# QKV's last two blocks: x transposed by VectorE and DMA transfers in place of TensorE

## What is computed

```python
x = x + attention(layernorm(x), Wqkv, bqkv, Wo, bo)     # q, k, v of width 256
x = x + ffn(layernorm(x), gate_w, up_w, down_w, fc1_w, fc2_w, expert_w, gamma, beta)
```

## Time and profile before

| | us |
|---|---|
| median of 3 runs | 2321.71 |
| lowest and highest | 2320.19 and 2321.98 |
| the profiled execution | 2322.11 |
| its span (first to last instruction) | 2320.3 |

### The profile page before, as it was taken

One profiled execution on the slowest core, in us unless ns is written; L12 is line 12 of the kernel. 1 busy time (PEld: TensorE's weight loads), 2 busy tenths in 40 slices (PEclk: granted clock), 3 DMA queues, 4 the chain that ended last, 5 costly groups with the idle time before them and its releaser, 6 DMA issues.

```text
span 2320.3 us, 27515 instructions
## 1 busy us (share of the span) xinstructions
PE 2307.1 (99%) x10888; PEld 1939.1 (84%) x10888; DVE 1578.0 (68%) x1772; ACT 794.3 (34%) x885; POOL 281.0 (12%) x550
## 2 busy tenths in 40 slices
PE   9999999999999999999999999999999999999998
PEld 8988988888888878888888888888888888888886
DVE  7787649887989765598763378774249876424548
ACT  4333336666555441522221331213132121223211
POOL 3000000000223200033100023210003220000000
PEclk9999999999999999999999999999999999999999
DMA  8999854532334699978996678898668999666865
GB/s 309 333 359 363 300 193 164 198 122 80 122 120 144 224 314 334 317 276 313 342 308 197 191 275 299 312 335 262 193 219 274 320 331 320 209 193 206 239 209 194
DMA packets 232801, 580.83 MB, mean 250 GB/s; under 512 B 26208, under 2 KB 80096, under 8 KB 232288
## 3 DMA queue, kind: packets, MB, share of 16 engines
q1 hardware_dynamic: 151392, 443.52, 58.1%
q10 hardware_dynamic: 81280, 135.55, 16.0%
HBM read 421.96 MB, written 152.83 MB: 248 GB/s over the span
## 4 chain that ended last, share of the span: by engine, by line
PE 92%; DVE 3%; DMA 1%; SPq 1%; ACT 1%; issue 1%; POOL 1%; ACTq 0%; DVEq 0%; POOLq 0%
PE psum L1116 11%; PE psum L1117 11%; PE psum L1118 11%; PE psum L1095 10%; PE psum L1096 10%; PE psum L1097 10%; PE psum L930 3%; PE psum L928 3%; PE psum L929 3%; PE psum L968 2%; PE psum L998 2%; PE psum L970 2%; PE psum L969 2%; PE psum L1000 2%; PE psum L999 2%; PE psum L948 1%
## 5 line engine op out<-in xcount | busy, mean ns | idle before, releaser
L1751 DVE TENSOR_TENSOR HB<-HB,psum 128x1024 f32<-128x1024 f32 x135 | 163.0, 1217 | 299.1 <-PE psum L1097 299.1
L1972 POOL TENSOR_SCALAR veA<-mvA 128x1 f32<-128x1 f32 x32 | 31.2, 976 | 1269.0 <-DVE mvA L1659 1269.0
L1341 ACT ACTIVATE HB<-HB 128x1024 f32<-128x1024 f32 x64 | 67.8, 1060 | 307.6 <-DVE HB L1751 307.6
L1095 PE MATMUL psum<-XS2h,WR 128*128 128x512 f32 x280 | 109.4, 391 | 1.0 <-DVE XS2l L1457 0.7
L1095 PE MATMUL psum<-XS1h,WR 128*128 128x512 f32 x280 | 109.3, 390 | 0.3 <-DMA WR<-wu_s 0.2
L1095 PE MATMUL psum<-XS0h,WR 128*128 128x512 f32 x280 | 109.1, 390 | 0.0
L1095 PE MATMUL psum<-XS3h,WR 128*128 128x512 f32 x280 | 109.1, 390 | 0.0
L1097 PE MATMUL psum<-XS0h,WR 128*128 128x512 f32 x280 | 109.0, 389 | 0.0
L1096 PE MATMUL psum<-XS1l,WR 128*128 128x512 f32 x280 | 109.0, 389 | 0.0
L1096 PE MATMUL psum<-XS2l,WR 128*128 128x512 f32 x280 | 109.0, 389 | 0.0
L1097 PE MATMUL psum<-XS1h,WR 128*128 128x512 f32 x280 | 109.0, 389 | 0.0
(11 more groups left out here) (402 smaller groups left out, 6616.6 us busy)
## 6 DMA issues: line engine op xcount, KB each, us to landing
WR<-wu_s SPq DMA_DIRECT2D x280, 512.0 KB, 4.3
WR<-wd_s SPq DMA_DIRECT2D x280, 512.0 KB, 4.7
att_s<-ATT ACTq DMA_DIRECT2D x32, 516.0 KB, 3.4
RAW<-in_x_dram SPq DMA_DIRECT2D x32, 512.0 KB, 8.2
RES<-x1b_s SPq DMA_DIRECT2D x128, 128.0 KB, 5.6
out_dram<-ZR ACTq DMA_DIRECT2D x118, 128.0 KB, 5.5
xT_s<-XT SPq DMA_DIRECT2D x24, 512.0 KB, 7.5
HB<-xT_s SPq DMA_DIRECT2D x12, 1024.0 KB, 8.8
```

The source lines that it names most:

```text
L1095: e.matmul(o, w[:, 0, ws], h[:, :, ws], start=kt == 0, stop=False)
L1751: e.tensor_tensor(to, a, src, op=ALU.add).then_inc(*vevac.next(key))
```

## The change

Blocks 6 and 7 (`MOVED`) no longer have `xt_tr`, `xt_hi` and `xt_lo`. In their place:

- `x_turn` (VectorE), four a block at slots b, b, b+1, b+1 with b = 12 (u - 1): transposes the 32x32 squares of one normalised tile of `RAW` into `XAT`, which is the memory of the low part of `XA[u % 2]`. It waits for the V products of block u - 2.
- `x_move` (SP) at b+2: 16 transfers of 32 partitions by 4 KB from `XAT` back into `RAW`, behind the last `x_turn`.
- `x_parts` at b+7 to b+10: high part (ScalarE) and low part (VectorE), read from `RAW` in runs of 32 numbers; both wait for all 16 transfers.

Since `RAW` is now in use until the last `x_parts`, all that waited for the last transpose of a block waits for its last low part (`raw_done`), and the quads d(1,0), d(1,1), d(2,0) and the loads and splits of q go one to three slots later. V's products of block 5 and 6 no longer wait for the transposes of the next block to be read out of their banks.

```diff
+MOVED = (6, 7)
@@ timetable
+        if u in MOVED:
+            for tt in range(4):
+                at(b + tt // 2, "x_turn", u, tt)
+            at(b + 2, "x_move", u)
+            for a in range(4):
+                at(b + 7 + a, "x_parts", u, a)
+            continue
         for a in range(4):
             at(b + 2 * a, "xt_tr", u, a)
             at(b + 2 * a, xt_out, u, a, b + 2 * a + 1)
-    for q, n0, times in ((("d", 1, 0), 68, (70, 71, 72, 72, 72, 73)), (("d", 1, 1), 75, (77, 78, 79, 79, 79, 80)),
-                         (("d", 2, 0), 82, (85, 86, 87, 87, 87, 88)), (("d", 2, 1), 84, (86, 87, 88, 88, 88, 89)),
+    for q, n0, times in ((("d", 1, 0), 71, (73, 74, 75, 75, 75, 76)), (("d", 1, 1), 78, (80, 81, 82, 82, 82, 83)),
+                         (("d", 2, 0), 85, (88, 89, 90, 90, 90, 91)), (("d", 2, 1), 84, (86, 87, 88, 88, 88, 89)),
...
-        at((80, 80, 86, 86)[j], "q_load_a", j // 2, j % 2)
-        at((84, 85, 89, 90)[j], "q_split_a", j // 2, j % 2)
+        at((83, 83, 88, 88)[j], "q_load_a", j // 2, j % 2)
+        at((86, 87, 90, 91)[j], "q_split_a", j // 2, j % 2)
@@ memory
+    XAT = [at(f"XA{i}t", [128, 4, 8, 4, 32], F32, 128.5 + 32 * i) for i in range(2)]
@@ ScalarE
+        def x_parts(u, a):
+            on.wait_ge(*xm_in[u])
+            src, h, _ = moved(u, a)
+            high(h, src, "xt", u, a)
@@ VectorE
+        def x_turn(u, tt):
+            on.wait_ge(*v_mm[u - 2, 3])
+            on.wait_ge(*normed[u, tt])
+            e.transpose(XAT[u % 2][:, :, :, tt, :].rearrange("p m k r -> p k m r"),
+                        RAW[u % 2][:, tt, :].rearrange("p (k m c) -> p k m c", k=8, m=4)).then_inc(*normed.next(("turn", u, tt)))
+
+        def x_parts(u, a):
+            src, h, l = moved(u, a)
+            low(l, src, h, "xt", u, a)
@@ SyncE
+        def x_move(u):
+            on.wait_ge(*normed["turn", u, 3])
+            for g, m in itertools.product(range(4), range(4)):
+                src = XAT[u % 2][32 * g:32 * g + 32, m].rearrange("p k t r -> p (k t r)")
+                e.dma_start(RAW[u % 2][32 * m:32 * m + 32, g, :], src).then_inc(
+                    *xm_in.next(*((u,) if g == m == 3 else ()), by=16))
```

More of the change, by code:

```diff
@@ L741, in transformer_layer @@
     wq_in, wv_in = [landed(f"wq{n}") for n in range(4)], landed("wv")
+    xm_in = landed("xm")
     bq_in, gr_in, bv_in = landed("bq"), landed("gr"), landed("bv")
@@ L802, in xt_bank, with raw_done, moved @@
         return 2 * (a % 2) if u == 0 else 6 - 2 * (a % 2)
+    def raw_done(u):
+        return lo["xt", u, 3] if u in MOVED else xt_mm[u, 3]
+    def moved(u, a):
+        src = RAW[u % 2][:, :, 256 * a:256 * a + 256].rearrange("p g (q r) -> p g q r", r=32)
+        return (src, *(q[:, 2 * a:2 * a + 2, :].rearrange("p k n -> p (k n)").rearrange("p (q g r) -> p g q r", q=8, g=4)
+                       for q in XA[u % 2]))
     def v_bank(t, tt):
@@ L939, in pe_v @@
             if t == 7:
-                on.wait_ge(*(vevac["v", 6, 3] if tt < 2 else lo["xt", 7, 2]))
-            elif tt < 2:
+                on.wait_ge(*(vevac["v", 6, 3] if tt < 2 else lo["xt", 5 if 7 in MOVED else 7, 2]))
+            elif tt < 2 or t + 1 in MOVED:
                 on.wait_ge(*(vevac["v", t - 1, tt] if t else lo["xt", 0, 3]))
@@ L1553, in P_acc @@
                 on.wait_ge(*exps[i, 1])
-                on.wait_ge(*(rs_mm[i - 1] if i else xt_mm[7, 3]))
+                on.wait_ge(*(rs_mm[i - 1] if i else raw_done(7)))
                 e.tensor_tensor(acc[:, :], SA[:, sa(i, 0), :], s, op=ALU.add).then_inc(*acc_s.next((1, i)))
@@ L1944, in vector @@
         do = {"e_split": e_split, "f_split": f_split, "wq_split": wq_split, "wv_split": wv_split, "load_qkv": load_qkv,
-              "ln_stats": ln_stats, "ln_norm": ln_norm, "e2_out": e2_out, "xt_lo": xt_lo, "v_out": v_out,
+              "ln_stats": ln_stats, "ln_norm": ln_norm, "e2_out": e2_out, "xt_lo": xt_lo, "x_turn": x_turn, "x_parts": x_parts, "v_out": v_out,
               "kv_split": kv_split, "q_split_a": q_split_a, "q_split": q_split, "mx_op": mx_op, "m_fold": m_fold,
@@ L2084, in q_load_a @@
             on.wait_ge(*qk_stored(i, d))
-            on.wait_ge(*(lo["q", i - 1] if i else xt_mm[7, 3]))
+            on.wait_ge(*(lo["q", i - 1] if i else raw_done(7)))
             e.dma_start(STQ[:, d, :], qk_s[i, d]).then_inc(*stq_in[d].next(i, by=16))
@@ L2124, in quad_load @@
             elif b == "qd":
-                on.wait_ge(*xt_mm[6, 3])
+                on.wait_ge(*raw_done(6))
             elif b == "qe":
@@ L2128, in quad_load @@
             elif b == "qc":
-                on.wait_ge(*xt_mm[7, 3])
+                on.wait_ge(*raw_done(7))
                 on.wait_ge(*lo["q", 1])
@@ L2319, in tail_out2 @@
                 e.dma_start(out[rows_].rearrange("p (a n) -> p a n", a=2)[:, cs], ZR[1][ps, cs, tt, :]).then_inc(*tail_st.next(by=16))
-        do = {"load_e": load_e, "load_f": load_f, "load_x": load_x, "load_qkv": load_qkv, "e2_out": e2_out,
+        do = {"load_e": load_e, "load_f": load_f, "load_x": load_x, "load_qkv": load_qkv, "x_move": x_move, "e2_out": e2_out,
               "kv_load": kv_load, "q_load_a": q_load_a, "q_load": q_load, "load_bo": load_bo, "load_wo": load_wo,
```

16 lines of the change are left out of this document (8 added, 8 removed).

## The result

| | median us | lowest to highest | runs |
|---|---|---|---|
| before | 2321.36 | 2320.19 to 2324.98 | 6 |
| after | 2336.61 | 2335.56 to 2339.61 | 6 |

The ratio is 1.0066, with a 95% interval of 1.0054 to 1.0078: the change costs 15.2 us. The forecast was +6.0 us, and the time lies just above the top of the range (2336). The profiled execution of the changed kernel took 2337.52 us, its span is 2335.7 us.

What follows compares the result with a forecast made beforehand. TensorE, busy 2307.1 of 2320.3 us, was taken as the bound. Transposes saved and three new waits, -7.1 + 8.1 + 1.0 + 4.0 = +6.0 us, gave 2327.7 us, range 2316 to 2336.

Steps and rivals of the forecast that it cites:

- the score products: After block 7: bias copies, q's splits and the store of d(2,0) come out level with TensorE; put at nothing.
- the third wait: Block 7: TensorE waits for low part (7,3), late behind x_move(7)'s issues and the store of d(1,0); 4 us taken.
- The transposes, -7.1 us: Blocks 6 and 7: 64 transposes leave TensorE in eight groups of 0.887 us, all on the path.
- The first wait, +8.1 us: Block 6: TensorE's 19th matmul waits for low part (6,3), until T + 2.9 us; 6.1 to 10.1 us.
- T: Landing of the last store of quad d(0,0), which K split 0 awaits; 253.8 us before, forecast 257.7 to 261.7.
- rival C: Transfers starve at 1.3 us an issue and land at 252.0 us; sum +10.0, 2331.7 us, up to 2336; chance 0.13.
- the twin's 0.67 us: Price of x_move's issues, from 16 transfers of the same size and direction that took 10.68 us on SyncE's queue.
- Slot 78, +1.0 us: Second wait: TensorE reaches bias copy (6,1) at T + 15.2, it ends at T + 16.2; between 0 and 2 us.
- The half clock: TensorE's clock might fall behind an 8 us wait, matmuls taking up to twice as long; counted in the upper end only.
- B (hidden transfers): Transfers fit in beside the stores and T stays at 253.8: -4.9 us, 2316.8 us; chance 0.25.
- D (one wait pays for all): While TensorE stands 8.1 us the others catch up and the later two waits are 0: +1.0, 2322.7 us; chance 0.12.
- A: The forecast's own sum of all terms, +6.0 us, with ends of 2320.7 to 2334.7 us; chance 0.50.

Runs made afterwards that it cites:

- the wide transfers: Changed kernel with x_move in 4 transfers of 128 partitions by 4 KB a block instead of 16 of 32 partitions, results wrong: 2329.61 us, ratio 1.0035.
- the filler: Changed kernel with 48 more transposes of the identity on TensorE between block 5 and block 6: 2343.87 us, ratio 1.0101.

## Why the prediction was wrong, step by step

The sum said +6.0 us, the terms measured above give +16.2. Of the 10.2 us between them, 5.8 are block 7 (forecast 4.0, measured 9.8), 3.6 are the score products (forecast 0) and 0.8 are block 6. The steps that failed are the third wait, with too few links and too cheap issues, and the score products, put at nothing without a working.

**The transposes, -7.1 us: right.** VectorE's and ScalarE's new work also cost what was forecast: a transpose of squares 1.22 us, a low part from SBUF 1.22, a high part 1.05. The pauses and the half clock less 7.1 give 16.2 us for a span that is 15.4 us longer. The run with one issue a block comes to the first score product 4.3 us early with 1.9 us of pauses on the way, which is 6.2 of the 7.1.

**The first wait, +8.1 us: right in size, in part by luck.** Block 6 lost 5.95 + 0.61 us of pauses and 2.35 of the half clock, 8.9. The chain that I worked out is real: T came at 261.03 us (forecast 257.7 to 261.7, taken 259.7), and TensorE's 19th matmul started at 263.92, T + 2.9 as forecast. With the wide transfers it was 257.65 and 260.54, from GpSimd 259.86 and 262.75: 2.9 each time. But the wait ahead of the first matmul was for the transfers themselves, landed at 254.28. The text named that as the point that would make it wrong ("landing after 252 us"), and only rival C had it, with 1.3 us for an issue; it was 1.42. In the changed kernel two things that the sum didn't have offset each other in T: the store of d(0,0) went out 11.2 us later than before (254.29 for 243.11), and landed 6.7 us behind its issue instead of 10.7. That T still fell into its range is luck. Where the issues were few, the working held: 257.65 with the wide transfers is the forecast's lower end (257.7), and 252.88 with one issue is near the 252.5 that its -1.3 us alone would give. One working is off besides: the higher upper end of 11 us for the transfers would move the middle, and so the sum, by 1 us and not by 2. What failed here is the price of an issue: the twin's 0.67 us was used, and the rows with long issues (5.16 us for four, rows 11; one by one 0.59, 0.60, 2.40 and 1.44) went into a rival of 0.13.

**Slot 78, +1.0 us: right.** 0.96 us.

**Block 7, +4.0 us: the term that was most under-sized.** It took 2.31 + 1.22 + 4.81 of pauses and 1.5 of the half clock, 9.8. The start of `x_move(7)` was right (T + 12.8 for T + 12.6), but it took 13.56 us and not 10.7, so that K split 7 and the store of d(1,0) came at T + 29.5 and not T + 26.6. And I looked only at low part (7,3). ScalarE's order in front of the *first* high part is K split 7, a bias copy, V split 0 and a second bias copy; it ran at 294.31, when TensorE had just ended V of block 6 (294.34). The largest wait (4.65 us) is at the third chunk, where VectorE does the sums of d(1,1), and its V low part waits 2.68 us for a V load: that load stands *behind* the load of d(1,1) in SyncE's queue, which waits for the store of d(1,0). The prediction followed d(1,1) to its sums and high parts, and left out the V loads behind it.

**The score products, 0: wrong, 3.6 us.** "Come out level" was not worked out. Lateness is not paid once and done: each quad's load waits for the store before it, so it is handed on. The slots themselves are innocent (2321.61 us with them alone) and even of use.

**The half clock, in the upper end only: partly wrong.** It came with the wait, with nearly twice the time for 11 matmuls, and once more in block 7, 3.9 us in all. In block 6 most of it lay over another wait.

**The rivals.** B (hidden transfers) is refuted by T at 261.03 us, 7 us behind its 254.1, and D (one wait pays for all) by the later waits of the changed kernel and by block 7 alone, which loses 12.5 us. C was nearest, 2331.7 and up to 2336. A and C together are what happened: their terms for block 6, plus a block 7 that neither had. The chances gave "slower" 0.48, the direction was right.

None of the kernels is faster than the kernel before beyond its interval. The one that comes nearest, with one issue a block, doesn't move x's squares, so it isn't a version of the kernel but shows what cheaper transfers could give with this timetable: about 2320 us. The kernel before stays the better one.

## What to carry to other kernels

Work that is taken from a bound engine and given to a transfer is paid in three places: the slots of the queue that issues it, the DMA engines, and every wait queued behind either. Price the issues by rows from a stretch as full, and from a row of issues as long, as those that they go to, and look at them one by one: a mean can hide a few long issues. And before a gain is booked, look at the stage behind it: if that is fed by a chain of loads and stores with its own pace, an engine that comes early waits there.

## What the runs showed of the hardware

- An issue of a small transfer from SBUF to SBUF isn't free: on SyncE 0.67 us each in the mean alone (rows 11), 0.85 in block 7 and 1.42 in block 6; with 128 bytes a partition still 0.71 and 0.98. The means mix issues of about 0.6 us with long issues of 1.1 to 2.4 us (1.0 to 1.4 with 128 bytes). The first four of block 6, and all four wide ones there, took 0.6 us beside full DMA engines. What the long issues wait for isn't shown; that the queue takes in only so many unfinished transfers would fit, and wasn't tested. From GpSimd an issue was 0.50 in the mean, but once it stood 6.49 us behind five of them.
- A faster issue isn't an earlier landing for what stands behind it: from GpSimd the first V load behind the transfers landed after 12.7 us (4.3 in the median of 270 to 300 us). The engines as a whole moved 208 to 222 GB/s while they were full of transfers of 32 partitions, half of the rate of rows 9; with 128 partitions they moved 389 in such a stretch. The Trainium skill (SBUF — State Buffer, "Door 1: The DMA port swizzle") has 189 GB/s for 32 partitions, measured with 1 MiB; these rows, with all other traffic in them, lie 10 to 17% above it.
- TensorE's clock fell from 2.4 to 1.2 GHz (grant 1.00 to 0.50) at 255.0 us, while it stood in the pause of 5.8 us, and 11 matmuls behind the pause ran at 0.43 us; in block 7 it fell at 306.2 us, just behind the pause of 4.65 us, for 6 matmuls. The length of a pause alone doesn't tell: it stayed up behind pauses of 2.15 and 1.8 us in the same kernel and of 2.46 with one issue, but fell behind one of 1.97 us in the run with block 7 alone (290.9 us) and one of 2.8 us with the filler (332 us). While TensorE did the transposes of the filler, and in the pause of 1.8 us behind them, the grant stayed at 1.00.
